# An attention layer on one core: the output bias added to the residual by GpSimd instead of by a TensorE product

## What is computed

```python
g   = group_norm(x)                                  # 32 groups
qkv = g @ qkv_w.T + qkv_b   (+ rank-4 additions to q and v)
a   = softmax(q k.T * scale + rel_h + rel_w)         # 12 heads of 64, 196 x 196 per image and head
out = x + (a v) @ proj_w.T + proj_b
```

## Time and profile before

| what | value |
|---|---|
| median of 3 runs | 3874.18 us (3871.25 to 3876.38) |
| profiled execution, its own time | 3877.42 us |
| its span, first to last instruction | 3875.7 us |
| PE, DVE, ACT, POOL busy | 93%, 67%, 54%, 1% |
| mean granted TensorE clock | 0.974 of full speed |
| one pair of images in the steady part | 115.7 us |

### The profile page before, as it was taken

How to read it: one execution, slowest core, us unless ns; L and a number is a source line. 1 busy time by engine, 2 the same in 40 slices (tenths; PEclk the granted TensorE clock), 3 DMA queues, 4 the chain that set the end, 5 groups by cost and what they waited for, 6 DMA issues and landing times.

```text
span 3875.7 us, 87367 instructions
## 1 busy us (share of the span) xinstructions
PE 3602.6 (93%) x33380; PEld 2407.7 (62%) x33380; DVE 2604.6 (67%) x6042; ACT 2089.0 (54%) x5651; POOL 34.0 (1%) x64
## 2 busy tenths in 40 slices
PE   5789999999999999999999999999999999999997
PEld 3456666666666666666666666666666666666665
DVE  6567666667666667667666666766766666766664
ACT  1455555555555555555555555655555555555553
POOL 0000000000000000000000000000000000000000
PEclk9899999999999999999999999999999999999998
DMA  4134434444444444444444444444444444444443
GB/s 111 31 75 81 92 83 91 85 83 80 92 83 90 85 85 87 84 92 86 86 79 88 83 89 87 86 85 89 80 90 86 90 78 88 82 89 86 90 73 78
DMA packets 789927, 326.88 MB, mean 84 GB/s; under 512 B 719555, under 2 KB 769731, under 8 KB 789454
## 3 DMA queue, kind: packets, MB, share of 16 engines
q1 hardware_dynamic: 773614, 283.28, 37.5%
q10 hardware_dynamic: 15840, 37.38, 3.8%
HBM read 86.61 MB, written 38.54 MB: 32 GB/s over the span
## 4 chain that ended last, share of the span: by engine, by line
PE 53%; DVE 20%; ACT 12%; issue 6%; DMA 5%; SPq 1%; POOL 0%; DVEq 0%; ACTq 0%; POOLq 0%
PE ring L602 27%; PE ring L678 13%; ACT prob L738 8%; PE score L651 5%; DMA rel_q<-rel_sb 5%; PE o_ps L665 4%; DVE split L851 4%; DVE row_max L828 3%; DVE rel_sb L820 3%; PE ring L609 2%; DVE rel_sb L814 2%; DVE stats L869 2%; DVE split L842 1%; DVE xT L799 1%; PE ring L686 1%
## 5 line engine op out<-in xcount | busy, mean ns | idle before, releaser
L602 PE MATMUL ring<-xn_hi,w_hi 128*128 128x392 f16 x3456 | 1166.5, 338 | 92.2 <-DVE rel_sb L820 87.2
L602 PE MATMUL ring<-xn_lo,w_hi 128*128 128x392 f16 x3456 | 1162.5, 336 | 0.0
L602 PE MATMUL ring<-xn_hi,w_lo 128*128 128x392 f16 x3456 | 1160.7, 336 | 0.0
L738 ACT ACTIVATE prob<-score,neg_max,exp_scale 98x196 f32<-98x196 f32 x1536 | 768.7, 510 | 616.2 <-DVE neg_max L832 612.5
L602 PEld LDWEIGHTS ring<-xn_hi,w_hi 128*128 128x128 f16 x3456 | 343.1, 99 | 374.5 <-DVE rel_sb L820 93.6
L851 DVE SCALAR_TENSOR_TENSOR split<-prob,row_inv,split 98x196 f16<-98x196 f32 x1536 | 546.1, 418 | 12.4
L837 DVE RECIPROCAL row_inv<-row_sum 98x4 f32<-98x4 f32 x384 | 68.4, 178 | 660.9 <-ACT prob L738 660.9
L678 PE MATMUL ring<-w_hi,o_lo 128*98 128x384 f16 x1536 | 502.4, 327 | 0.0
L678 PE MATMUL ring<-w_hi,o_hi 128*98 128x384 f16 x1536 | 502.4, 327 | 0.0
L678 PE MATMUL ring<-w_lo,o_hi 128*98 128x384 f16 x1536 | 502.2, 327 | 0.0
L602 PEld LDWEIGHTS ring<-xn_hi,w_lo 128*128 128x128 f16 x3456 | 344.8, 100 | 248.9 <-issue 21.6
(11 more groups left out here) (125 smaller groups left out, 5400.0 us busy)
## 6 DMA issues: line engine op xcount, KB each, us to landing
y_sb<-in_x SPq DMA_DIRECT2D x256, 147.0 KB
out<-y_sb SPq DMA_DIRECT2D x256, 147.0 KB
x_sb<-in_x ACTq DMA_DIRECT2D x31, 1176.0 KB
rel_q<-rel_sb SPq DMA_DIRECT2D x128, 147.0 KB, 7.1
stage<-in_L_conv_qkv_w SPq DMA_DIRECT2D x3, 2304.0 KB, 19.0
turned<-split SPq DMA_TRANSPOSE x384, 4.0
stage<-in_L_conv_proj_w SPq DMA_DIRECT2D x1, 2304.0 KB, 20.3
x_sb<-in_x SPq DMA_DIRECT2D x1, 1176.0 KB
```

What stands on the lines that cost most here:

```text
L602: last = T.matmul(ring[:, bank, 0:NT], w[:, c, 128 * j:128 * j + 128], xx[:, t.par, c, :], start=(c == 0 and part == 0), stop=(c == CT - 1 ...
L738: last = A.activation(prob[:, step[3], head, half, :], score[0:HALF, head, TOK * half:TOK * half + TOK], ACT.Exp, bias=neg_max[:, step[3], ...
```

## The change

`bias_rows` becomes a float32 tile of 98 equal rows, filled by one load that repeats `proj_b` over 98 partitions. The scaling, the splitting and the zeroing of it are gone, and so is the first product of each Y piece. In its place GpSimd has a step B for each of the 8 pieces: it waits until the residual has been loaded, adds the bias to it in `y_sb`, and signals `biased`. DVE's step Y waits for `biased` where it waited for the load. In GpSimd's order, B 4 to 7 (of the pair before) and then B 0 to 3 (of this pair) stand behind its one small operation. In `prepare`, GpSimd waits for the bias load ahead of its reduction over partitions.

```diff
-POOL_ORDER = each("G", -1, 1)
+POOL_ORDER = each("G", -1, 1) + each("B", 1, 4, 5, 6, 7) + each("B", 0, 0, 1, 2, 3)
...
-        ones = sb(keep, "ones", [128, HALF], BF16)
-        bias_rows = sb(keep, "bias_rows", [128, C], BF16)
+        bias_rows = sb(keep, "bias_rows", [HALF, C], F32)
...
-            act.wait_ge(brow_zeroed, 1)
-            for limb in range(3):
-                act.dma_start(brow[32 * limb:32 * limb + 1, :],
-                              g["proj_b"].rearrange("(a c) -> a c", a=1)).then_inc(brow_in, 16)
+            act.dma_start(g["bias_rows"][:, :], g["proj_b"].partition_broadcast(HALF)).then_inc(brow_in, 16)
...
+            pool.wait_ge(brow_in, 16)
             pool.wait_ge(maxima, 1)
...
-            V.memset(brow[:, :], 0.0).then_inc(brow_zeroed, 1)
-            V.memset(g["ones"][:, :], 1.0)
-            V.memset(g["bias_rows"][:, :], 0.0)
...
-            dve.wait_ge(brow_in, 48)
-            step(V.tensor_scalar(brow[:, :], brow[:, :], inv[:, 3:4], inv[:, 2:3], ALU.mult, ALU.mult))
-            for limb in range(3):
-                step(V.tensor_copy(brow16[:, limb, :], brow[:, :]))
-                if limb < 2:
-                    step(V.tensor_tensor(brow[:, :], brow[:, :], brow16[:, limb, :], ALU.subtract))
-                row = slice(32 * limb, 32 * limb + 1)
-                V.tensor_copy(g["bias_rows"][row, :], brow16[row, limb, :])
...
-                        T.matmul(to, ones[:, :], bias_rows[:, out_c], start=True, stop=False)
                         for c in range(HP):
                             for part, (w, oo) in enumerate(((w_hi, o_hi), (w_hi, o_lo), (w_lo, o_hi))):
                                 last = T.matmul(to, oo[:, o_slot(t.par, c), tok], w[:, c, 3 * C:][:, out_c],
-                                                start=False, stop=(c == HP - 1 and part == 2))
+                                                start=(c == 0 and part == 0), stop=(c == HP - 1 and part == 2))
...
+                    elif step[0] == "B":
+                        t, k = turn.of(step[1]), step[2]
+                        wait(pool, y_in[k % 4], 32, t.q, 16 * (k // 4) + 16)
+                        G.tensor_tensor(y_sb[:, k % 4], y_sb[:, k % 4], bias_rows[:, YC * (k % 2):YC * (k % 2) + YC],
+                                        ALU.add).then_inc(biased, 1)
...
                         wait(dve, done[kind], YS, t.q, k + 1)
-                        wait(dve, y_in[k % 4], 32, t.q, 16 * (k // 4) + 16)
+                        wait(dve, biased, YS, t.q, k + 1)
```

More of the change, by code:

```diff
@@ L251, in prepare @@
         tmp = sb(own, "tmp", [128, 1], F32)
-        brow = sb(own, "brow", [128, C], F32)
-        brow16 = sb(own, "brow16", [128, 3, C], BF16)
         mask = sb(own, "mask", [128, 1], F32)
@@ L259, in prepare @@
         lora_in, small_in = sem("lora_in"), sem("small_in")
-        brow_zeroed, brow_in = sem("brow_zeroed"), sem("brow_in")
+        brow_in = sem("brow_in")
         merged, lora_done = sem("merged"), sem("lora_done")
@@ L480, in attend @@
     onehot = g["onehot"]
-    ident, gmean, bias, ones, bias_rows = g["ident"], g["gmean"], g["bias"], g["ones"], g["bias_rows"]
+    ident, gmean, bias, bias_rows = g["ident"], g["gmean"], g["bias"], g["bias_rows"]
     exp_scale, neg_scale, rel_scale, rel_hi_scale, y_scale = (
@@ L525, in attend @@
         o_ps = own.enter_context(nc.psum_tensor("o_ps", [128, 512], F32))
+        biased = sem("biased")
         y_in = [sem(f"y_in{i}") for i in range(4)]
```

## The result

The change made the kernel slower: 3918.28 us (median of 4 runs, 3913.15 to 3926.98) against 3875.28 us before (4 runs), ratio 1.011, 95% interval 1.0081 to 1.0138. The forecast was 3844 us with a range to 3912 us. It was wrong in sign, and the time lies 6 us outside the range, in the case with a chance of 0.29: DVE and GpSimd take turns (3914 us, 3885 to 3930).

The account below looks back on a forecast made before the run. PE alone bounds one stage of each pair; transfer, softmax and norm the other. Savings 25.2 + 1.3 + 4.0 = 30.5 us, adds 0: 3874.2 - 30.5 = 3843.7, say 3844 us; own range 3838 to 3850, 8 in 10 3836 to 3912.

Parts of the forecast that it names:

- DVE and GpSimd take turns: End of PE's stage: DVE waits for the rest of one add and two whole ones, 2.2 us per pair; chance 0.29.
- What bounds the kernel, and what the product saves: PE alone paces the stage holding Y 3 to 7: 0.81 us saved per pair, 25.2 us, plus 1.3 us in the last.
- The 115.7 us of the prediction: The time after which the chain repeats, one pair, read as 1745.52 less 1629.85.
- `prepare`: Before the pairs: without the bias work `w_lo` starts 4.8 us earlier; the new load takes back 0.8, leaving 4.0 us.
- The length of an add: GpSimd's add of 384 elements: 0.87 us, estimated from a selection row, with bounds of about 0.7 and 1.59 us.
- The place of the adds: Adds 0 to 3 run from about 1742.8 to 1746.4, while DVE has unit 8's softmax remainders from 1744.05 to 1745.97.
- The adds in time: Adds finish well before DVE wants their Y pieces, so its new wait on `biased` is hidden everywhere.
- The step that failed: Adds beside DVE's unit 8 operations: 0 us per pair taken as likeliest, upper end about 2.4 us; no meeting 0.38.
- The rival: The case that DVE and GpSimd take turns: 70 us back in all, 3914 us (3885 to 3930); chance 0.29.
- The upper bound of 2.4 us: Most that adds 0 to 3 cost per pair at unit 8: 0.65 + 2 x 0.87 us of DVE waiting.
- Held once per pair: DVE waits only for the add under way at 1744.05: 0.45 us mean, 14.4 us back, 3858 us (3845 to 3871); chance 0.26.
- Adds 4 to 7: In PE's stage they meet like DVE work; 1.81 us of DVE slack and PE's pace cover about their cost.

Follow-up runs that it names:

- The removal alone: The changed kernel without the eight adds, DVE waiting for the load itself, bias left out of the result: 3841.88 us, ratio 0.9909 against the kernel before.
- adds behind R: The changed kernel with adds 0 to 3 held until DVE has read the next pair's first R piece: 3845.18 us, ratio 0.9924 against the kernel before.
- The fill: The changed kernel with each add replaced by a one-element sum and a 768-element scratch fill, bias left out: 3859.0 us, ratio 0.996 against the kernel before.
- the copy: The changed kernel with each add replaced by a one-element sum and a 768-element copy of `bias_rows` into scratch, bias left out: 3893.74 us, ratio 1.0044.
- the kernel with every add placed: The changed kernel with adds 0 to 3 behind R, 4, 5, 7 behind negated maxima, 6 behind the last `xn_lo`, bias load later: 3840.56 us, ratio 0.9911.

## Why the prediction was wrong

- **What bounds the kernel, and what the product saves: right.** The removal alone took 32.3 us off, where 30.5 were worked out. Per pair, from the first to the last `rstd` over 31 distances, it is (3654.6 - 120.0) / 31 = 114.02 us before and (3626.0 - 115.3) / 31 = 113.25 us with the removal alone: 0.77 us, where 0.81 were taken. The 115.7 us of the prediction are those of one pair, longer than the mean.
- **`prepare`: 3.2 us instead of 4.0 in the profiled execution.** The first `w_lo` starts at 76.98 us instead of 80.23. In the experiments with the same preparation it starts at 76.2 to 80.4 us, and in the one that keeps the old one at 81.84 us, against 80.23 us before. So it varies by some microseconds with the same code, and neither the exact saving nor a push of the weights by the new load is shown.
- **The length of an add: 1.00 us, not 0.87** (990 to 1256 ns over 256 of them, median 1000). The bounds 0.7 and 1.6 us held it. In plain proportion the 4497 ns for 2048 elements that the prediction takes from the Trainium skill (GPSIMD Engine Reference, section 3.1) give 0.84 us for 384, not 0.9: an estimate under the measured length too. The place of the adds was right: the prediction had the first one start 1.25 us ahead of the first copy of unit 8. It starts 1.3 us ahead in one of the two pairs above, together with it in the other, and the four meet all of L830 and one or two of the four L839.
- **The adds in time: right.** DVE never waits for `biased` in the list of waits; adds behind R cost nothing.
- **The step that failed** is the sentence "For the likeliest case I take 0 us, since the rows show no meeting and an operation held back". No row showed a meeting, but also none in which the two engines read SBUF together and did *not* disturb each other. Zero was the bound, and it was taken as the value. The same text had what speaks for the other end: the place, the missing slack (k_lo ends where q_lo starts), and the rule that it cites from the Trainium skill. The measured cost of adds 0 to 3 is 2.2 us of holding per pair, and 73 / 32 = 2.3 us of time. The rival had 0.45 + 2 x 0.87 = 2.2 us. The upper bound of 2.4 us, which takes 0.65 us for the rest of an add where its own words allow 0.87, held in the mean, but not in each pair: the one shown has 2.93 us.
- **The rival's mechanism: right in kind, a little different in form.** It had DVE wait for two whole adds behind the one under way. The rows have four adds without a gap, with DVE doing about one operation of 0.3 to 0.4 us per 1.0 us of add, so each add in a row costs some 0.7 us. The figures are 2.93 / 4 = 0.73 us in the pair shown, and 1.24 - 0.55 = 0.69 us for the single one. That the rival's sum fits so well is in part luck: it had fewer holdings, each of a whole add.
- **"Held once per pair" falls** for the changed kernel: DVE is held beside each of the four adds, not once. The kernel that leaves a single add there is the one whose time, 3851.5 us, lies in this case's 3845 to 3871.
- **Adds 4 to 7: right in what they cost.** They held DVE for 67 us in all, and the cover named for them (1.81 us of slack at Y 6) was enough within the uncertainty: 3845.2 us with them, 3841.9 us without.

The page that the prediction cites for this is SBUF — State Buffer in the Trainium skill; its section is "Who interferes with whom", and "The single rule" is a line in it. It states that a VectorE operation with two SBUF inputs contends with a GpSimd operation that reads SBUF and not with one that only writes it, and that one in a two-port mode contends with either. The fill and the copy agree with it. In numbers, as means over the whole kernel: with fills 418 ns, with copies 456 ns, with adds 461 ns for the line with two inputs, and 363, 353 and 412 ns for the one with one, against 418 and 320 ns before. That the loser "fully blocks", for a whole instruction as the prediction has it, is not borne out by the recorded starts and lengths. From 1641.38 to 1645.65 four adds and four DVE operations get through, 4.27 us for what would take 3.85 and some 1.3 us one behind the other; and the first L830, which is held, had started 0.03 us ahead of the first add. Whether an add's record also holds time in which it doesn't use SBUF isn't shown. That L830 runs in such a two-port mode is an inference from this, not a reading.

## What to carry to other kernels

GpSimd's idle time isn't free by itself: here its work held VectorE's operations that read only SBUF, and cost time where the chain went over them. Before moving an elementwise operation there, list what VectorE executes in the stretch in which the moved one will run, and read its slack there, not its busy share; the operation's start is set by the transfer or semaphore ahead of it, so one more wait can put it beside work that reads PSUM, where it cost nothing here. When a trace doesn't show two resources used together, its silence is no reason for the lower bound.

## What the runs showed of the hardware that was not expected

- In the changed kernel GpSimd hardly pays. Four adds beside DVE's operations of 0.3 to 0.4 us took 4.02 us, against 3.85 us for four beside the R operations, while the same six DVE operations took 4.90 us instead of 1.97 us. Longer DVE work did hold it: in the kernel with every add placed, an add that starts beside `xn_lo` (0.97 us, two SBUF inputs) took 1.65 us.

```profile
1568.31 1.65 POOL L771 TENSOR_TENSOR y_sb<-y_sb,bias_rows 98x384 f32<-98x384 f32 x1 [7.35 <-DVE neg_max L827]
```

In the kernel with the copies a sum of one element, 0.19 us alone, took 2.11 us beside a row of DVE operations that all read SBUF, and ended 0.05 us behind the last of them, an `xn_lo`. DVE lost nothing (GpSimd, then DVE, in order of time):

```profile
1587.07 2.11 POOL L767 TENSOR_TENSOR tiny<-minus_half 98x1 f32<-98x1 f32 x1 [8.80 <-DMA y_sb<-in_x]
```

```profile
1586.04 1.42 DVE L842 SCALAR_TENSOR_TENSOR split<-prob,row_inv,split 98x196 f16<-98x196 f32 x4
1587.38 0.87 DVE L885 TENSOR_SCALAR xT<-xT,mean,rstd 128x392 f32<-128x392 f32 x2
1588.17 0.96 DVE L891 TENSOR_TENSOR xn_lo<-xT,xn_hi 128x784 f16<-128x784 f32 x1
```

What decides which of the two is held isn't shown.

- A fill, which reads nothing, still nearly doubles L830: 1.02 us for two instead of 0.56 us.
- 67 us of holding in PE's stage cost 3 to 6 us of time, no more than the uncertainty, and 70 us in DVE's stage cost 73. The same event is free or paid in full by its place alone.
